# Edge counts out of the short units of the self stage, two waits and two copies moved in the FFN, and the first x tile loaded in two halves (one-core graph layer)

## What is computed

```python
xn = _layernorm(x, axis=-1)                       # x is 1250 x 1024, float32
x = x + gnn(xn, src, dst, ...) + mix(xn[None], ...)[0]
x = x + ffn(_layernorm(x, axis=-1)[None], w1, w2)[0]

# gnn: two layers over 20000 edges
msg = h[edge_src]
agg = jax.ops.segment_sum(msg, edge_dst, num_segments=h.shape[0])
mean = agg * deg_inv[:, None]
h = relu(h @ W_self0 + mean @ W_neigh0 + b0)      # layer 0; layer 1 the same, without relu
# mix: linear attention with relu(q), relu(k), v, 16 heads, then @ Wo
# ffn: two linear layers (1024 -> 4096 -> 1024) with gelu between, rows quantised to
#      integers of -128..127, weights to -1, 0, 1
```

## Time and profile before

| | us |
|---|---|
| median of 3 runs (1287.69 to 1288.70) | 1288.04 |
| the profiled execution | 1288.82 |
| span of its trace, first to last instruction | 1287.0 |
| TensorE (PE) busy | 1280.6 |
| VectorE busy | 877.1 |
| ScalarE busy | 664.2 |
| GpSimd busy | 96.3 |
| granted TensorE clock, mean | 1.000 |

### The profile page before, as it was taken

How to read it: one execution, slowest core, us unless ns; L and a number is a source line. 1 busy time by engine, 2 the same in 40 slices (tenths; PEclk the granted TensorE clock), 3 DMA queues, 4 the chain that set the end, 5 groups by cost and what they waited for, 6 DMA issues and landing times.

```text
span 1287.0 us, 19572 instructions
## 1 busy us (share of the span) xinstructions
PE 1280.6 (100%) x6544; PEld 628.5 (49%) x6544; DVE 877.1 (68%) x1529; ACT 664.2 (52%) x938; POOL 96.3 (7%) x91
## 2 busy tenths in 40 slices
PE   9999999999999999999999999999999999999999
PEld 5454445555544445555444554444444444444444
DVE  6954452455567768897992994427877978786674
ACT  7765564556412336443433664547853376565460
POOL 0000000000000001110000100323540000000000
PEclk9999999999999999999999999999999999999999
DMA  9488988566335465645876448599949829732533
GB/s 359 147 266 262 296 256 228 204 230 235 110 115 195 152 209 172 204 139 198 280 249 222 139 131 261 153 353 259 315 133 376 262 74 294 181 68 66 131 61 103
DMA packets 170486, 260.36 MB, mean 202 GB/s; under 512 B 76192, under 2 KB 111776, under 8 KB 166816
## 3 DMA queue, kind: packets, MB, share of 16 engines
q1 hardware_dynamic: 158400, 251.36, 60.1%
q0 software_dynamic: 1440, 5.24, 2.2%
q10 hardware_dynamic: 10560, 2.62, 1.8%
HBM read 184.87 MB, written 57.55 MB: 188 GB/s over the span
## 4 chain that ended last, share of the span: by engine, by line
PE 93%; DMA 2%; DVE 2%; ACT 1%; issue 1%; ACTq 1%; DVEq 0%; SPq 0%
PE ps L2479 26%; PE ps L2839 14%; PE ps L2956 9%; PE ps L2919 9%; PE ps L2744 8%; PE ps L2612 8%; PE ps L2791 7%; PE ps L2809 7%; PE ps L2685 2%; DMA STREAM<-in_w1t 1%; ACTq L958 1%; PE ps L2622 1%; PE ps L2531 1%; PE ps L2513 1%; ACT S L979 1%
## 5 line engine op out<-in xcount | busy, mean ns | idle before, releaser
L2479 PE MATMUL ps<-S,XH 128*128 128x512 f16 x960 | 209.0, 379 | 0.0
L2479 PEld LDWEIGHTS ps<-S,XH 128*128 128x128 f16 x960 | 93.6, 98 | 110.9
L2479 PE MATMUL ps<-S,Zb 128*128 128x512 f16 x480 | 106.7, 379 | 0.0
L2744 PE MATMUL ps<-XH,S 128*128 128x512 f16 (+1 forms) x576 | 105.7, 339 | 0.0
L2612 PE MATMUL ps<-XH,S 128*128 128x512 f16 (+1 forms) x576 | 102.6, 339 | 0.0
L2479 PE MATMUL ps<-Zb,XH 128*128 128x512 f16 x432 | 94.8, 379 | 0.0
L1827 DVE TENSOR_SCALAR STREAM<-tables,keys 128x320 f16 x222 | 67.3, 303 | 34.2 <-issue 17.4
L1152 ACT ACTIVATE AT<-ps 128x320 f16<-128x320 f32 x40 | 17.4, 435 | 139.8 <-PE ps L2479 83.8
L2791 PE MATMUL ps<-XH,AT 128*128 128x512 f16 x400 | 86.7, 379 | 0.0
L2809 PE MATMUL ps<-AT,Zb 128*128 128x512 f16 (+1 forms) x480 | 84.7, 339 | 0.0
L2612 PEld LDWEIGHTS ps<-XH,S 128*128 128x128 f16 x576 | 56.1, 98 | 45.7
(11 more groups left out here) (346 smaller groups left out, 2149.5 us busy)
## 6 DMA issues: line engine op xcount, KB each, us to landing
STREAM<-in_w_all SPq DMA_DIRECT2D x48, 512.0 KB, 5.3
STREAM<-in_w1t SPq DMA_DIRECT2D x42, 512.0 KB, 5.1
STREAM<-in_w2t SPq DMA_DIRECT2D x28, 512.0 KB, 5.7
XIN<-in_x SPq DMA_DIRECT2D x20, 512.0 KB, 5.7
Zb<-in_w1t SPq DMA_DIRECT2D x14, 512.0 KB, 7.4
blocks_scratch<-S SPq DMA_DIRECT2D x4, 1792.0 KB, 8.6
blocks_scratch<-STREAM SPq DMA_DIRECT2D x4, 1792.0 KB, 8.5
S<-blocks_scratch SPq DMA_DIRECT2D x7, 1024.0 KB, 11.3
```

The lines of the kernel that those rows point to most:

```text
L2479: last = mm(acc[:, n * BANK:(n + 1) * BANK], left(l, kc), right(kc, r)[:, n * BANK:(n + 1) * BANK], start=(kc == 0 and i == 0), stop=(kc = ...
L2744: last = mm(acc[:, n, :], W[:, kc, r, (c + 4 * n) * P:(c + 4 * n + 1) * P], XH[:, l, kc, unit_cols(u)], start=(kc == 0 and i == 0), stop=( ...
```

## The change

The counts are distributed otherwise: the tenth step of the u stage gets three parts instead of two, wide units of the self stage three each, short units none. The sum over AT of unit 2 moves to unit 5, and the first quad of the stage from unit 0 to unit 1. In the FFN TensorE's wait for the four block sums is split in two and moved behind the first products; VectorE's integers of tile 8 go behind the first two sums of G = 2; from p = 2 on ScalarE copies the P1 products of the odd G before and after the last gelu of the even G. At the start x tile 0 comes as columns 0 to 511 by SP (semaphore `deg_in`) and columns 512 to 1023 by ScalarE's queue (`x_in0`), its statistics wait for each half apart, and ScalarE's root for tile 1 comes one piece later.

```diff
-PARTS = [1] * 4 + [2] * 6 + [2, 2, 1, 3, 2, 1, 3, 3, 1, 3, 3, 1]
+PARTS = [1] * 4 + [2] * 5 + [3] + [3, 3, 0] * 4
...
-SUMS_AT = {2: (0,), 5: (1,), 8: (2,), 11: (3,)}
+SUMS_AT = {5: (0, 1), 8: (2,), 11: (3,)}
...
+            if G > 3 and G % 2 and step == "P1" and s == 0:
+                return 14 * G
+            if G > 3 and G % 2 == 0 and step == "10" and s == 1:
+                return 14 * G + 15
...
-        S0_QUADS = {0: 0, 2: 1, 3: 2, 5: 3, 6: 4, 8: 5, 9: 6}
+        S0_QUADS = {1: 0, 2: 1, 3: 2, 5: 3, 6: 4, 8: 5, 9: 6}
...
-            load_x(0, 0)
+            sp.dma_start(XIN[:, 0, 0:BANK], rows(x, 0)[:, 0:BANK]).then_inc(S("deg_in"), 16)
...
+            nc.scalar.dma_start(XIN[:, 0, BANK:D], rows(x, 0)[:, BANK:D]).then_inc(S("x_in0"), 16)
             act.wait_ge(S("eps"), 1)
             A(col("f_z1"), col("eps"), ACT.Sqrt)
             ln_std(0)
...
                 square(0, kc)
-                if kc == 3:
+                if kc == 4:
                     ln_std(1)
...
-                for s in range(2):
-                    f1_copy(G, s, 1 + s, 0, 0, 8 * p - 4)
+                if p < 2 or g == 0:
+                    for s in range(2):
+                        f1_copy(G, s, 1 + s, 0, 0, 8 * p - 4)
...
                 for s in range(2):
+                    if p > 1 and g == 0 and s == 1:
+                        f1_copy(G + 1, 0, 1, 0, 0, 8 * p - 4)
                     act.wait_ge(S("f1_d"), 6 * G + 5 + s)
                     alone(act)
                     gelu(t + 1, 0, 2 * g + s)
+                if p > 1 and g == 0:
+                    f1_copy(G + 1, 1, 2, 0, 0, 8 * p - 4)
...
-                dve.wait_ge(S(f"x_in{j}"), 8 * (t - j) + 16)
+                whole = not (isinstance(t, int) and t == 0)
+                if whole:
+                    dve.wait_ge(S(f"x_in{j}"), 8 * (t - j) + 16)
                 wait(dve, "ln_lo", t)
                 for n in range(2):
+                    if not whole:
+                        dve.wait_ge(S(("deg_in", "x_in0")[n]), 16)
...
-            x2_ints(8, 0)
-            f1_dve(1, 0, later(lambda: None), later(lambda: None), later(x2_scaled, 9))
+            f1_dve(1, 0, later(x2_ints, 8, 0), later(lambda: None), later(x2_scaled, 9))
...
                 if g == 0:
                     for j in range(2):
                         pe.wait_ge(*x2T_in(2 * p + j, j))
-                    pe.wait_ge(S("x2_sums"), 4 * p + 4)
...
                     f1_product("P2", p, G, s, 1)
+                    pe.wait_ge(S("x2_sums"), 4 * p + 3)
                     pe.wait_ge(S("f1_act"), f1_done(G, "P1", s))
                     f1_product("P6", p, G, s, 0, False, False)
...
+                pe.wait_ge(S("x2_sums"), 4 * p + 4)
                 for s in range(2):
                     pe.wait_ge(S("f1_act"), f1_done(G, "P5", s))
                     f1_product("P3", p, G, s, 0, False)
```

More of the change, by code:

```diff
@@ L629, in quad_load @@
                     sp.wait_ge(S("h_sq"), UNITS)
-                    sp.wait_ge(S("deg_in"), 32)
+                    sp.wait_ge(S("deg_in"), 48)
                 if i == RING_QUADS:
@@ L709, in _ @@
                 .then_inc(S("deg_in"), 16)
-            sp.wait_ge(S("deg_in"), 16)
+            sp.wait_ge(S("deg_in"), 32)
             sp.dma_start(inv_deg, deg_d.partition_broadcast(P)).then_inc(S("deg_in"), 16)
@@ L1856, in counts_dve @@
                 parts = list(parts_of(tile))
-                count_dve(parts[0])
+                for part in parts[:1]:
+                    count_dve(part)
                 between()
@@ L2017, in h_rows @@
                 if u == 0:
-                    dve.wait_ge(S("deg_in"), 32)
+                    dve.wait_ge(S("deg_in"), 48)
                 wait(dve, "h_sq", u - COL_PARTS + 1)
@@ L2693, in counts_between @@
                 parts = list(parts_of(tile))
-                places = {1: (7 if tile == 0 else 6,), 2: (3, 6), 3: (2, 4, 6)}[len(parts)]
+                places = {0: (), 1: (7 if tile == 0 else 6,), 2: (3, 6), 3: (2, 4, 6)}[len(parts)]
                 def at_place(kc):
```

## The result

| | before | changed |
|---|---|---|
| median of 7 runs each, us | 1287.78 (1287.65 to 1288.70) | 1292.64 (1292.07 to 1293.63) |
| the profiled execution, us | 1288.82 | 1293.63 |
| span of its trace, us | 1287.0 | 1291.8 |

The change costs 4.9 us: the ratio is 1.0035, with a 95% interval of 1.0025 to 1.0045. The forecast was 1288.4 with a range up to 1290.2, so both the number and the range were wrong. The two spans (first to last instruction) differ by 4.8 us, and the traces have all of it.

The account below looks back on a forecast made before the run. The prediction took TensorE to bound the kernel (1280.6 of 1287.0 us busy), so only its stalls could change. Its terms, -0.1 - 1.24 + 2.2 + 0.25 - 0.79 = +0.3 on 1288.04, gave 1288.4 us, range 1285.4 to 1290.2.

Parts of the forecast that it names:

- The start: Loading x tile 0: TensorE's earlier start is lost again before tile 2; only a slightly earlier last Wk piece counts, -0.1 us.
- The blocks of the short units and of unit 10: Self stage: five TensorE stalls in count blocks of units 2, 5, 8 and 10 go, -1.24 us.
- Unit 1: Self stage: no stall forecast; units not named had at least 0.15 us to spare on VectorE.
- Unit 3: First count block: TensorE waits for one-hot rows behind the moved first quad on VectorE, +2.2 us (0 to 3.1).
- T2: Zero point for the first quad's times: the start of short unit 2 on TensorE.
- Unit 6: First count block: two sums in a row on VectorE in unit 5 make its rows late, +0.25 us (0 to 0.5).
- The FFN: TensorE's stops for the block sums (0.40) and for ScalarE's copy of P1 (0.39) go, -0.79 us.
- The quad costs nothing: Rival, chance 0.20: the first quad's 2.2 us stall in unit 3 isn't there, giving 1286.1 us.
- the start is kept: Rival, chance 0.12: up to 1.2 us of the earlier start stays; without the quad's stall too, 1285.0 us.
- nothing but order: Rival, the rest of the "same" cases: FFN edits only move waits to the next product, -0.8 becomes 0, 1289.2 us.
- a late half tile: Rival, chance 0.07: x tile 0's second half lands near 10.6 us instead of 4.5, +6.1 us, 1294.

Follow-up runs that it names:

- e12: Kernel before with only the start edit (x tile 0 in two halves, split statistics wait, later root): 1288.56 us, ratio 1.0000.
- e4: Changed kernel with two parts of counts in unit 0 instead of three, and three instead of two in the ninth u step: 1291.94 us, ratio 1.0027.
- e10: Changed kernel with VectorE reading early only the bounds of a wide unit's first count part: 1291.94 us, ratio 1.0030.
- e6: Changed kernel with the sum over AT of unit 5 back in unit 2: 1292.88 us in a single run.
- e1: Kernel before with only the change's three tables (counts, sums over AT, quads) and small edits letting a unit have no part: 1294.12 us, ratio 1.0040.
- e8: Changed kernel with VectorE reading the bounds of all the self stage's count parts into registers ahead of need: 1292.89 us, ratio 1.0035.
- e5: Changed kernel with 12 matmuls of zeros added just ahead of unit 3's first count block: 1292.61 us, ratio 1.0036.
- e2: Changed kernel with the three tables of before, so the start and FFN edits alone: 1287.58 us, ratio 0.9991.
- e3: Changed kernel with the first quad back in unit 0: 1289.64 us, ratio 1.0009.
- e7: As e2, but with VectorE's integers of tile 8 back in their old place: 1287.79 us, ratio 0.9997.
- e9: Changed kernel with first quad in unit 0, sum in unit 2, e4's parts and tile 8's integers in their old place: 1287.33 us, ratio 0.9993.
- e11: As e9, but with three parts in unit 0 as in the change and e10's early bounds: 1288.14 us, ratio 0.9999.

## Why the prediction was wrong, point by point

- **The start** (-0.1 forecast). Nothing that can be told from chance: e12's trace has the start of before, and the 0.33 us of the changed kernel's lies within what varies from one execution to the next, as first transposes lie between 6.96 and 7.42 us in the twelve traces with the halves (mean 7.19) and at 7.25 and 7.29 in the two without. "DMA: Bandwidth & Descriptors" of the Trainium skill, section "Issuing engines are not separate DMA queues", says that DMAs issued by two engines save the sequencer's time only; the trace agrees, as in e12 the first statistics start at 4.52 us, before at 4.53. The reason that the prediction gave for the small number was false, though, and its -0.1 was right by luck. The last Wk piece did come earlier, by far more than 0.1 (its square starts at 15.85 in place of 17.00, in e12 at 16.13, and by 16.23 in ten of the twelve traces with the halves), and it gained nothing. Nor is an earlier start given back: the restart follows the first transposes by 20.2 to 20.3 us in all fourteen traces, by 20.21 before, in the changed kernel and in e12. The chain of waits shows why: it runs through TensorE's own matmuls behind those transposes and not through the square of the last piece.
- **The blocks of the short units and of unit 10** (-1.24). Right in all its places: the five stops are gone (1.1 us by the table's measure). That they came from TensorE's sequencer stays argued; no run tests it.
- **Unit 1** (forecast: nothing). This is the step that failed. The prediction costed a part of counts on VectorE at two iterations, 0.83 + 0.75 us, from the part that stands behind a long sum at 495.92 in the earlier trace rows, where no gap shows. The third part in unit 0 costs 3.3 us, of which 1.7 are gaps. The chain of small operations for the scales follows it, so that no long operation covers the next part's start either, and TensorE lost 1.8 us (e4 and e10). The gaps were there to be read in the trace of before (478.19, above), in a stretch of which no rows were taken. "The other units have at least 0.15 us to spare by the same sum" was the sentence: the sum was the wrong one.
- **Unit 3** (+2.2). The mechanism was right to 0.05 us up to VectorE's end: roundings at T2 + 3.99, quad done at T2 + 6.43, first rows ready at T2 + 8.95 (the prediction's own terms add up to 8.91 and not 8.96, which changes nothing). The term was too small by 0.6, since TensorE takes up its work 0.18 us after the first iteration is ready and 0.38 after the second (503.13 to 503.31, 503.89 to 504.27), and has 0.2 more at the end of the block.
- **The clock** (not forecast). +1.3 us in the trace, about 0.9 net, in the two of seven executions that have it; the median execution does not. Behind its start, no stop of the kernel before is over 0.6 us, so its trace could not show it.
- **Unit 6** (+0.25). Right place and cause (e6), 0.85 measured. VectorE was late by 0.31, where 0.22 had been worked out; the rest is TensorE's restart (0.39 behind VectorE's end) and 0.2 at the end of the block, as in unit 3.
- **The FFN** (-0.79). Both stops gone, as forecast. That VectorE's integers of tile 8 move had no price in the prediction: 0.5 us of new wait in this trace.
- **The rivals.** "The quad costs nothing", "the start is kept" and "nothing but order" went the wrong way, though the second was right in that tile 2's normalisation doesn't hang on the last Wk piece; there was only nothing to keep. The slower one, a late half tile, had the right sign and the wrong mechanism: all of the loss is in the tables, where the forecast saw +1.2 net and e1 measures 6.0.

In sum: -0.1 - 1.24 + 2.2 + 0.25 - 0.79 = +0.3 should have read, for the profiled execution, 0 - 1.1 + 1.8 (unit 1) + 2.8 + 1.3 (clock) + 0.85 - 0.3 = +5.35; the trace shows 4.8, with -0.4 in the start's column and -0.2 in that of the k, v stages, which no edit explains. Unit 1 is the largest term that was missing, but it alone would have given 1290.2, the very end of the range; the restarts of units 3 and 6 (0.6 each) and the FFN's new wait (0.5) carry it beyond. The medians differ by 4.9 without any fall of the clock in them.

## What to carry to other kernels

A loop driven by registers had gaps of 1.17 to 1.26 and about 0.46 us here where no long operation stood in front of it, and none behind operations of 1.2 us: price such a loop by its slowest appearance in the trace, and look at what will stand ahead of it after the change. When work is gathered into fewer places, follow each in-order engine through the place that gets more, not only through the one that is emptied. And where a stop of TensorE has been worked out, add its restart, 0.2 to 0.4 us for each wait here, and look at the clock of every execution, not only of the profiled one.

## What was not expected of the hardware

- The granted clock fell behind stops of 1.9 and 0.7 us, but only in part of the executions of one and the same kernel: the mean clock (three decimals are on record) is 0.999 in 2 of 7 of the changed kernel, 5 of 5 of e1, 5 of 9 of e4, the one of e6, 2 of 5 of e8 and 3 of 7 of e10, and 1.000 in the others, in all five of e5, where the wait is filled, and in every one on record of the kernels without this stop (before, e2, e3, e7, e9, e11, e12). Five of these traces show the fall at unit 3 (changed, e1, e6, e8, e10). Stops in unit 1 aren't needed for it, by e4's executions. What decides between two executions of one kernel is open.
- Slower matmuls behind a stop give VectorE time to catch up: without them (the traces of e4 and e5) a stop of 0.4 us appeared one unit later.
- An x tile loaded in halves by two engines is in no sooner than whole by one: in e12 the statistics' two operations start at 4.52 and 5.13 us, before at 4.53 and 5.14.
